# First cross attention of a four-layer kernel: exact scores in three double visits, plain scores partly four heads at a time, a queue of three batches

## The reference

```python
q = x @ w_q + b_q                    # x: [32, 112, 256], after its layernorm
k = context @ w_k + b_k              # context: [32, 375, 192]
v = context @ w_v + b_v
# 16 heads of 16
scores = jnp.einsum('bqhd,bkhd->bhqk', q, k) * scale
weights = jax.nn.softmax(scores, axis=-1)
out = jnp.einsum('bhqk,bkhd->bqhd', weights, v).reshape(B, Lq, D)
return out @ w_o + b_o
```

## Time and profile before

| | us |
|---|---|
| Median of 3 runs | 2233.82 |
| The three runs | 2224.35, 2233.82, 2236.61 |
| The profiled execution | 2225.22 |
| Its span | 2223.4 |
| Its TensorE clock, mean share granted | 0.972 |
| Busy over the span: PE, DVE, ACT, POOL | 2050.3, 1412.7, 1035.3, 891.6 |

### The profile page before, as it was taken

How to read it: one execution, slowest core, us unless ns; L and a number is a source line. 1 busy time by engine, 2 the same in 40 slices (tenths; PEclk the granted TensorE clock), 3 DMA queues, 4 the chain that set the end, 5 groups by cost and what they waited for, 6 DMA issues and landing times. The chain is left out here.

```text
span 2223.4 us, 61979 instructions
## 1 busy us (share of the span) xinstructions
PE 2050.3 (92%) x21235; PEld 1670.6 (75%) x21236; DVE 1412.7 (64%) x3682; ACT 1035.3 (47%) x2466; POOL 891.6 (40%) x1479
## 2 busy tenths in 40 slices
PE   5999999999879999959999999959999999999996
PEld 4777777777657777748999999947777777777774
DVE  4666667666448888854333233226787887878785
ACT  2444444444334444423233233226666666666663
POOL 3444444444136666640000000025656566666651
PEclk9999999999889999979999999969999999999998
DMA  6222232225050000021111111120111111101010
GB/s 183 80 77 77 79 96 83 77 77 202 2 164 18 25 21 21 23 77 32 35 35 38 36 35 38 35 86 21 36 30 35 30 35 30 37 28 39 26 29 9
DMA packets 98790, 118.81 MB, mean 53 GB/s; under 512 B 9778, under 2 KB 91442, under 8 KB 98610
## 3 DMA queue, kind: packets, MB, share of 16 engines
q1 hardware_dynamic: 92594, 103.43, 15.3%
q0 software_dynamic: 6144, 14.69, 2.2%
HBM read 67.36 MB, written 50.72 MB: 53 GB/s over the span
## 5 line engine op out<-in xcount | busy, mean ns | idle before, releaser
L1263 ACT ACTIVATE e_act_T<-ps_quad,fc_b 128x128 f32<-128x128 f32 x504 | 136.8, 383 | 313.3 <-PE ps_quad L1328 313.3
L479 DVE TENSOR_REDUCE a_negmax<-ps_turned 112x2 f32<-112x750 f32 x256 | 240.0, 938 | 59.8 <-PE ps_turned L569 58.5
L1328 PEld LDWEIGHTS ps_quad<-e_xT,e_w_now 128*128 128x128 f32 x2016 | 236.6, 193 | 7.9 <-DVE e_xT L1297 4.1
L1328 PE MATMUL ps_quad<-e_xT,e_w_now 128*128 128x128 f32 x2016 | 237.6, 276 | 3.5 <-DVE e_xT L1297 3.5
L422 ACT ACTIVATE a_probsT<-ps_quad 125x896 f32<-125x896 f32 x192 | 176.2, 918 | 128.0 <-PE ps_quad L581 123.7
L1343 PE MATMUL ps_out<-w,e_act_T 128*128 x1008 | 228.1, 379 | 0.8 <-DVE e_y L1305 0.8
L1441 POOL COPY c_index<-slot 112x1 uint32 (+1 forms) x64 | 19.4, 332 | 477.8 <-POOLq L1226 477.8
L1343 PEld LDWEIGHTS ps_out<-w,e_act_T 128*128 128x128 f32 x1008 | 186.6, 190 | 24.0 <-issue 1.2
L1294 DVE COPY e_w_now<-w 128x2048 f32 x63 | 77.3, 1227 | 200.4 <-PE ps_quad L1328 190.5
L1468 POOL TENSOR_TENSOR c_kL<-c_kT,c_kH 128x376 fp32r<-128x376 f32 x128 | 126.5, 988 | 169.3 <-ACT c_kH L1520 168.7
L206 ACT ACTIVATE c_probs<-ps_quad,c_negmax 112x375 f32<-112x375 f32 x256 | 144.0, 571 | 26.8 <-DVE c_negmax L167 26.8
(11 more groups left out here) (304 smaller groups left out, 5287.5 us busy)
## 6 DMA issues: line engine op xcount, KB each, us to landing
slots<-a_zeros SPq DMA_DIRECT2D x60, 512.0 KB, 5.0
a_cT<-in_ctx_t SPq DMA_DIRECT2D x32, 375.0 KB, 3.6
c_cT<-in_ctx_t SPq DMA_DIRECT2D x32, 375.0 KB, 3.2
w<-in_fc_t SPq DMA_DIRECT2D x2, 4096.0 KB, 21.7
w<-in_fc_t SPq DMA_DIRECT2D x8, 1024.0 KB, 11.8
e_xg<-slots SPq DMA_DIRECT2D x63, 128.0 KB, 2.0
slots<-e_y SPq DMA_DIRECT2D x63, 128.0 KB, 1.7
out<-c_fo SPq DMA_DIRECT2D x32, 112.0 KB, 1.9
```

The costliest lines, as they stand in the source:

```text
L479: dve.tensor_reduce(negmax[:, t, e, :].rearrange("p (r c) -> p r c", c=32)[:, 2 * half:2 * half + 2, 0], plain[0:T, :, 0:CTX], AX, ALU.max ...
L1263: last = act.activation(act_T[par][:, c * TILE:(c + 1) * TILE], hidden[par][:, c // 4, (c % 4) * TILE:(c % 4 + 1) * TILE], ACT.Gelu, bias= ...
L1328: last = pe.matmul(hidden[par][:, c // 4, (c % 4) * TILE:(c % 4 + 1) * TILE], w1_now[:, k, c * 128:(c + 1) * 128], xT[par][:, k, :], start ...
```

## The change

- Each step is written in a new order on all engines, and one batch further apart: step b now ends batch b, makes the scores of batch b + 1, the projections of batch b + 2 and (POOL, DVE) the context split and moments of batch b + 3. The written-out steps at both ends become more.
- The six visits become three: `scores(of, i)` fills two chunks side by side in the four banks of `quad` with 32 matmuls, and one exp of 4 x 448 columns (1,792 elements a partition) reads both. `probsT` is one tile of six chunks.
- Of the eight plain units of a batch, four become two: `plain_scores(of, t, 0)` writes four heads into the four banks of `quad`, and DVE takes four maxima in one instruction over 1,500 elements a partition. `quad` is now shared between exact and plain scores; the other four units stay pairs in `plain`.
- `v_product(0)` and `(1)` go to the two halves of `proj` and are copied by one DVE instruction (512 columns).
- The load of x is in three parts instead of two.

```diff
-def over_batches(eng, step, before=1, after=1, first=2):
+def over_batches(eng, step, before=1, after=1, first=2, last=2):
...
-    with eng.Fori(first // 2, NB // 2 - 1) as i:
+    with eng.Fori(first // 2, (NB - last) // 2) as i:
...
-    for b in range(NB - 2, NB + after):
+    for b in range(NB - last, NB + after):
...
-        probsT = [sb(f"probsT{i}", [KC, 3, 4, HALF]) for i in range(2)]
+        probsT = sb("probsT", [KC, 6, 4, HALF])
...
-                sp.dma_start(residual[0:T, 2:NB, :], w["x"].rearrange("b t d -> t b d")[:, 2:NB, :]).then_inc(x_in[1], 16)
+                sp.dma_start(residual[0:T, 2:6, :], w["x"].rearrange("b t d -> t b d")[:, 2:6, :]).then_inc(x_in[1], 16)
+                sp.dma_start(residual[0:T, 6:NB, :], w["x"].rearrange("b t d -> t b d")[:, 6:NB, :]).then_inc(x_in[2], 16)
...
-                def exp(b, t, c):
-                    act.wait_ge(scores_ready, 6 * b + 3 * t + c + 1)
-                    wait(act, values_ready, 2 * (b - 1) + t + 1)
-                    act.activation(probsT[t][:, c, :, :], turned[0:KC, :, 0:HALF], ACT.Exp).then_inc(exp_ready, 1)
+                def exp(b, i):
+                    act.wait_ge(scores_ready, 3 * b + i + 1)
+                    wait(act, values_ready, 2 * (b - 1) + (1 if i == 0 else 2))
+                    act.activation(probsT[:, 2 * i:2 * i + 2, :, :].rearrange("p c r x -> p r c x"),
+                                   quad[0:KC, :, 0:2 * HALF].rearrange("p r (c x) -> p r c x", c=2), ACT.Exp).then_inc(exp_ready, 1)
...
+                def maximum(b, at, t, e, half=None):
+                    dve.wait_ge(plain_ready, 6 * b + at)
+                    rows = negmax[:, t, e, :].rearrange("p (r c) -> p r c", c=32)
+                    if half is None:
+                        dve.tensor_reduce(rows[:, :, 0], quad[0:T, :, 0:CTX], AX, ALU.max, negate=True).then_inc(max_ready, 1)
+                    else:
+                        dve.tensor_reduce(rows[:, 2 * half:2 * half + 2, 0], plain[0:T, :, 0:CTX], AX, ALU.max, negate=True)\
+                           .then_inc(max_ready, 1)
...
+                def v_copy_first(b, to):
+                    dve.wait_ge(v_mm, 2 * b + 2)
+                    dve.tensor_tensor(v[to][:, 0:2, :, 0:HD], proj[0:KC, :].rearrange("p (c h d) -> p c h d", c=2, h=H),
+                                      bv[0:KC, :].rearrange("p (h d) -> p h d", h=H).unsqueeze(1).to_broadcast([KC, 2, H, HD]), ALU.add)\
+                       .then_inc(v_ready, 1)
...
+                    def plain_scores(of, t, e, half=None):
+                        for r in range(4) if half is None else (2 * half, 2 * half + 1):
+                            rows = slice(32 * r, 32 * r + 32)
+                            to = quad[0:T, r, 0:CTXE] if half is None else plain[0:T, r % 2, 0:CTXE]
+                            last = pe.matmul(to, qH[of][rows, t, e, :], kH[of][rows, t, :], start=True, stop=True)
                         last.then_inc(plain_ready, 1)
+                    def scores(of, i):
+                        for half in range(2):
+                            t, c = divmod(2 * i + half, 3)
+                            keys = slice(c * KC, (c + 1) * KC)
+                            for term in range(4):
+                                for r in range(4):
+                                    rows = slice(32 * r, 32 * r + 32)
+                                    left, right = ((ones[rows, 0:KC], shift[rows, t, :]),
+                                                   (kH[of][rows, t, keys], qH[of][rows, t, :, :].rearrange("p e t -> p (e t)")),
+                                                   (kL[of][rows, t, keys], qH[of][rows, t, :, :].rearrange("p e t -> p (e t)")),
+                                                   (kH[of][rows, t, keys], qL[of][rows, t, :, :].rearrange("p e t -> p (e t)")))[term]
+                                    last = pe.matmul(quad[0:KC, r, half * HALF:(half + 1) * HALF], left, right, start=(term == 0), stop=(term == 3))
                         last.then_inc(scores_ready, 1)
...
+                        pe.wait_ge(exp_ready, 3 * b + 2)
+                        scores(par, 2)
+                    if exists(nxt):
+                        pe.wait_ge(max_ready, 6 * nxt + 2)
+                        plain_scores(1 - par, 0, 1, 0)
+                    if exists(b):
+                        pe.wait_ge(v_ready, 2 * b + 2)
+                        wait(pe, o_biased, b)
+                        values(par, 0)
+                    if exists(nxt):
+                        if exists(b):
+                            pe.wait_ge(exp_ready, 3 * b + 3)
+                        plain_scores(1 - par, 0, 0)
+                        pe.wait_ge(max_ready, 6 * nxt + 3)
+                        plain_scores(1 - par, 1, 1, 1)
+                    if exists(later):
+                        pe.wait_ge(c_split, 2 * later + 2)
                         if exists(nxt):
+                            pe.wait_ge(v_ready, 2 * nxt + 2)
+                        k_product(0)
+                    if exists(b):
+                        pe.wait_ge(exp_ready, 3 * b + 3)
+                        values(par, 1)
+                    if exists(nxt):
+                        pe.wait_ge(max_ready, 6 * nxt + 4)
+                        plain_scores(1 - par, 1, 0)
+                    if exists(later):
+                        pe.wait_ge(k_whole, 2 * later + 1)
+                        k_product(1)
...
+                        pe.wait_ge(k_ready, 2 * nxt + 2)
+                        pe.wait_ge(shift_ready, 2 * nxt + 2)
+                        pe.wait_ge(exp_ready, 3 * nxt + 1)
+                        scores(1 - par, 1)
                     if exists(later):
+                        pe.wait_ge(q_high, later + 1)
+                        pe.wait_ge(k_high, 2 * later + 1)
+                        if exists(nxt):
+                            pe.wait_ge(shift_ready, 2 * nxt + 2)
+                        plain_scores(par, 0, 1, 1)
+                        pe.wait_ge(q_whole, later + 1)
+                        v_product(0)
+                        v_product(1).then_inc(v_mm, 1)
+                        pe.wait_ge(k_high, 2 * later + 2)
+                        pe.wait_ge(max_ready, 6 * later + 1)
+                        plain_scores(par, 1, 1, 0)
+                over_batches(pe, step, 3, 1, 2, 4)
```

More of the change, by code:

```diff
@@ L276, in cross_first @@
         ident, psum = mem["ident"], mem["psum"]
-        proj, outs, turned, plain = psum["proj"], psum["out"], psum["quad"], psum["turned"]
+        proj, outs, quad, plain = psum["proj"], psum["out"], psum["quad"], psum["turned"]
         norm = Norm(nc, ctx, "a_norm", mem)
@@ new lines, in step @@
+                    if exists(later):
+                        k_copy(later, 1)
+                    if exists(nxt):
+                        shift_copy(nxt, 0)
+                    if exists(later):
+                        act.wait_ge(xT_mm, later + 1)
+                        wait(act, q_mm, later)
+                        act.activation(xT[:, :, :].rearrange("p k t -> p (k t)"), plain[:, 1, 0:HALF], ACT.Copy).then_inc(xT_ready, 1)
+                    if exists(b):
+                        act.wait_ge(oT2_mm, b + 1)
@@ L457, in _ @@
-                over_batches(act, step, 2, 1)
+                        shift_copy(nxt, 1)
+                        exp(nxt, 0)
+                        exp(nxt, 1)
+                over_batches(act, step, 3, 1, 2, 4)
             @block.vector
@@ L572, in scores @@
[L572 to L581 removed]
+                        to = proj[0:KC, D:2 * D] if c == 1 else proj[0:KC, 0:D]
@@ new lines, in step @@
+                    if exists(nxt):
+                        pe.wait_ge(max_ready, 6 * nxt + 5)
+                        shift_turn(0)
+                    if exists(later):
+                        pe.wait_ge(norm.rows_ready, later + 1)
+                        for k in range(2):
+                            last = pe.transpose(plain[:, 1, k * T:(k + 1) * T], xn[:, k * 128:(k + 1) * 128], ident[0:T, 0:T])
+                        last.then_inc(xT_mm, 1)
+                        pe.wait_ge(k_whole, 2 * later + 2)
+                        v_product(2).then_inc(v_mm, 1)
@@ L697, in step @@
-                    if exists(later):
-                        pe.wait_ge(norm.rows_ready, later + 1)
-                        if exists(b):
-                            pe.wait_ge(xT_ready, nxt + 1)
-                        for k in range(2):
-                            last = pe.transpose(plain[:, 1, k * T:(k + 1) * T], xn[:, k * 128:(k + 1) * 128], ident[0:T, 0:T])
-                        last.then_inc(xT_mm, 1)
-                over_batches(pe, step, 2, 1)
+                        pe.wait_ge(k_ready, 2 * nxt + 2)
```

285 lines of the change are left out of this document (88 added, 197 removed).

## The result

| | before | changed |
|---|---|---|
| Median, us | 2235.22 (4 runs, 2224.35 to 2236.73) | 2172.20 (4 runs, 2170.73 to 2178.35) |
| Profiled execution, us | 2225.22 | 2170.73 |
| Its clock, mean share granted | .972 | .971 |
| A step of the first stage, mean | 17.55 | 15.80 |
| End of the first stage (its last POOL instruction) | 609.5 | 546.0 |

The changed kernel takes 0.973 of the time of before (95% interval 0.971 to 0.976), 63 us less by the medians. The range of 8 in 10 (2136 to 2176) held the time; the forecast's own band (2136 to 2164) did not. Most of the forecast gain is there; some 20 us went to one wait that no term of the sum had.

What follows compares the result with a forecast made beforehand. PE was taken to bound the first stage: work 14.29 plus waits .76 make 15.05 us a step, against 17.55. The stage loses 76 us: 2225.2 - 76 = 2149, plus 5 to 6, 2154; 8-in-10 range 2136 to 2176.

Steps and rivals of the forecast that it cites:

- Bound and direction: First stage: PE, busy 496.88 of 526 us, sets the step; the step falls from 17.55 to 15.05 us.
- PE's own work, 14.29: PE's step without waits: 15.56 before, less .95 for five fewer shape changes and .32 for two pairs, 14.29 us.
- a change of shape: PE switching between whole-array and 4 x 32 matmuls costs .19 us, whatever is ready; 16 a step before, 11 after.
- Sizes of the wide reads: PSUM reads on ACT and DVE: wide exp 1.66 us, maximum over 1,500 elements 1.71, copy of two v chunks .69.
- rival 2: Wide exp and maximum take twice the single rows (1.84, 1.88): +.46 a step, 14 us, 2168 us; chance .09.
- The four new waits, .76: PE waits at third visit .15, next plain pair .28, first quartet .11, last v product .12; .76 with the loop's turn.
- The loop's turn: Every second step PE's wait at the loop's turn, .36, replaces the third visit's wait: + .10 us on average.
- The rest has slack: the second quartet comes .6 after the maximum it needs: PE waits nowhere else: second quartet .6 us after its maximum, shift turnings 1.4 and .5 after theirs.
- Around the steps: First stage's head and tail: step 1 begins near 64, last two steps 24 us plus 6 for the clock; end 530 to 534.
- From the profile to the median: Whole kernel: profiled execution 2225.2 - 76 = 2149 us, plus 5 to 6 for the median, 2154.
- Rival 3: The shared `quad` ring decides and is slower: at an exp of 2.8 us, step 18.15, +18 us, 2249; chance .03.
- The signs: Profile marks: step 15.0 to 15.2 us, exps 1.66, maxima 1.71, quartet .26 to .36, four PE waits only, end near 532.

Runs made afterwards that it cites:

- the version with the apply moved: Changed kernel with the layernorm's apply on DVE done one step earlier, behind the rounding of q, where POOL is idle; 2151.13 us, 0.966 of before.

## Why the prediction was right, and where it was wrong

- **Bound and direction: right.** PE sets the step before and after, and the gain is what leaves PE's order.
- **PE's own work, 14.29: right within .1.** It is not measured by itself: 15.10 less the waits below leave 14.37. The price of a change of shape is shown (.18). The quartet costs PE .27 from start to start in the mean against .26 for a pair; the .05 more that the prediction weighed against its rows is not there.
- **Sizes of the wide reads: right.** 1.67 for exp, 1.71 to 1.72 for the maximum, .68 for the copy of v; rival 2 falls.
- **The four new waits, .76: in their places, and right within .03.** PE's timeline of the version with the apply moved, read as in the prediction, over two steps:

```profile
288.79 1.36 PE L587 MATMUL ps_out<-a_probsT,a_v 125*32 125x112 f32 x48
290.29 0.43 PE L565 MATMUL ps_quad<-a_kH,a_qH 32*112 32x376 f32 x4
...
295.12 0.35 PE L638 MATMUL ps_turned<-ident,a_xn 112*128 112x112 f32 x2
295.62 0.28 PE L258 MATMUL ps_proj<-a_wvL,a_cH 128*125 128x256 f32 x1
...
302.20 0.42 PE L565 MATMUL ps_turned<-a_kH,a_qH 32*112 32x376 f32 x2
302.49 0.37 PE L579 MATMUL ps_quad<-a_shift,a_ones 32*125 32x224 f32 x4
...
303.36 0.27 PE L579 MATMUL ps_quad<-a_qL,a_kH 32*125 32x224 f32 x4
303.66 0.42 PE L565 MATMUL ps_turned<-a_kH,a_qH 32*112 32x376 f32 x2
304.01 1.36 PE L587 MATMUL ps_out<-a_probsT,a_v 125*32 125x112 f32 x48
305.40 0.43 PE L565 MATMUL ps_quad<-a_kH,a_qH 32*112 32x376 f32 x4
...
310.23 0.35 PE L638 MATMUL ps_turned<-ident,a_xn 112*128 112x112 f32 x2
310.65 0.28 PE L258 MATMUL ps_proj<-a_wvL,a_cH 128*125 128x256 f32 x1
```

  First quartet: 288.79 to 290.29 is 1.50, in the next step 304.01 to 305.40 is 1.39, and 1.29 passes without a wait: .21 and .10, in the mean .15 (said .11). Last v product: 295.12 to 295.62 is .50, in the next step 310.23 to 310.65 is .42, against .19 for two turnings and .12 for the first product: .19 and .11, in the mean .15 (.12). Third visit: .29 between the starts, less the pair's .16: .13, in the mean of all steps .14 (.15). Next plain pair: .30 to the start and .10 for its load, less .11: .29 (.28). The loop's turn is in these means: the steps take 15.02 and 15.20 in turn, and most of the difference stands at the first quartet and the last v product, not at the third visit, where the prediction put its .10. Together .73. That leaves 14.37 for PE's work, .08 more than said, and the waits are .03 less than said: together the .05 between 15.05 and 15.10. Where the .08 lie is not shown.
- **The step that failed: "The rest has slack: the second quartet comes .6 after the maximum it needs".** The slack is real (.67), but the sum laid out DVE's order with the apply at .41, its duration where POOL was idle. In its new place POOL is in the middle of its work, and the maximum starts some 1.3 late: .6 of slack gone and .6 to .7 of wait in its place. Another .08 a step stand at the turning back of the output, where the prediction had said that there is hardly any slack on DVE: from the shift turning ahead of it to the visit behind it PE takes .55 in the mean, and .48 with the apply moved. In the loop's steps the two make .74, over all 29 steps .70 in the mean, 20 us in all. The prediction said of POOL that it has 7.4 us of work a step and "is asked for it late", and of the context split that it moved "past nothing that PE waits for". It looked at who waits for POOL's results, and not at who works beside POOL. The rows to see it were in the trace of before, in its first microseconds, where one apply of the 32 takes 1.13 us. DVE and POOL there:

```profile
17.21 1.13 DVE L245 TENSOR_SCALAR a_xn<-residual,a_norm_moments,a_norm_rstd 112x256 f32<-112x256 f32 x1 [0.94 <-POOL a_norm_rstd L240]
```
```profile
17.26 0.93 POOL L371 CAST a_cH<-a_cT 128x376 fp32r<-128x376 f32 x2
```

- **Around the steps: some 6 us too much.** Step 1 begins at 60.8 (said 64), and from the end of the 29 steps to the end of the stage are 26.9 (said 30). With these and 15.10 a step: 60.8 + 437.9 + 27.3 = 526, the measured end with the apply moved. With 15.80: 546. (The prediction's own figures differ a little here: its sum gives 530.5, which is 79 under 609.5, and it went on with 76.)
- **From the profile to the median.** 2149.2 was forecast for a profiled execution and 2170.7 came: 12.5 more by the stage (63.5 us saved, not 76), 8.6 by the stages behind, .4 outside the profile's span. The 5 us that the prediction added for the median were too few beside the 8.6: the profiled execution of before was a short one in just the stages that nobody touched, and the sum was made against it.
- **The range held by luck in part.** The time lies above the forecast's band (2136 to 2164) and in the part that was added for rival 2, whose price was 2168. The cause of rival 2 did not come: exp and maximum took 1.67 and 1.71. The wait behind the apply, which stands nowhere in the prediction, happened to cost 20 us, beside its 14.
- **Rival 3** was not met. Its figures don't agree: at an exp of 2.8, .3 for each .1 beyond 1.7 gives 18.35, not 18.15.
- **The signs** were well chosen. "PE idle at the third visit, at the pair behind it, at the first quartet and at the last v product, .1 to .3 each, and nowhere else" was the one that told: the view of waits shows the second quartet. DVE late at the turning back of the output, named among what would be wrong, came too, with .08.

## What to carry to other kernels

When an order is changed, note for every DVE instruction that goes from SBUF to SBUF (copy, cast, tensor_scalar) what POOL does in its new place, and keep such an instruction out of POOL's runs, or give it to ACT; its old duration holds only with POOL idle. It shows in a profile as a long duration, not as a wait, so look for one form of instruction whose minimum and maximum lie far apart before and after. And profile the old kernel twice before half a per cent in stages that nobody touched is read as an effect of the change.

## What the runs showed of the hardware

- DVE's apply over 112 x 256 from SBUF to SBUF takes .41 us beside an idle POOL and 1.29, 1.93 or 2.3 beside a busy one, each time till about .15 us behind the last instruction of POOL's unbroken run. In the changed kernel that run ends with a pause of .09, and the apply came through though POOL then went on. One cast was let in after one of two POOL instructions (1.14 instead of .39). Where the apply started ahead of POOL's instruction, it took .40 and POOL's 1.25 instead of 1.14. ACT's takes .59 beside the same run. Maxima that read PSUM are not stretched.
- With one wait of PE of 1.5 us in each step of a stage that is else dense, the granted clock fell to 1.2 GHz in 4 steps of 30, every sixth, for some 7 us, and cost 3 us each time.
- One more change of the array's shape in a step (a plain pair between a k product and the values) cost PE .18 us.
- Two executions of one and the same program differ by 12 us in the stages behind the first, while its first stage repeats within .4.
